# Eight fused layers on one core: work moved across the barriers before the second and third attention, and no announcements of free banks

## The reference

```python
x = x + L0_xattn(layernorm(x), ctx, ctx, Wq, Wk, Wv, Wo)       # 32 heads
x = x + L0_ffn(layernorm(x), c1_w, c2_w, w1, w2t)              # one row per block of 32
x = x + L1_xattn(layernorm(x), ctx, Wq, Wk, Wv, Wo)            # 16 heads of 96, keys: context and x
x = x + L1_ffn(layernorm(x), W, b, lora_A, lora_B)             # Hadamard rotation, LoRA
x = x + L2_xattn(layernorm(x), ctx, mask, Wq, Wk, Wv, Wo, qn, kn)   # 32 heads of 128, q and k normed
x = x + L2_ffn(layernorm(x), weight)                           # quantised to fp8
x = x + L3_xattn(layernorm(x), ctx, ctx)                       # autocorrelation
x = x + L3_ffn(layernorm(x), w1, s1, w2, s2, w3, s3)           # packed 4-bit weights
```

## Time and profile before

| | before |
|---|---|
| median of 3 runs | 1517.04 us (1515.98 to 1517.22) |
| profiled execution, its own time | 1517.68 us |
| its span | 1516.0 us |
| mean granted TensorE clock | 0.968 of full speed |
| TensorE busy | 1394.9 us (92%) |
| VectorE busy | 1078.9 us (71%) |
| ScalarE busy | 763.0 us (50%) |
| GpSimd busy | 719.9 us (47%) |
| DMA | 174.63 MB, q1 59.4% of 16 engines |

### The profile page before, as it was taken

The page is one execution under the profiler, slowest core; times in us unless marked ns, Lnnn a source line. Parts: engine busy times, 40 slices in busy tenths (PEclk is TensorE's granted clock), DMA queues, the critical chain, the costliest instruction groups (busy, mean ns, idle before and its releaser), DMA issues. The chain is left out here.

```text
span 1516.0 us, 31472 instructions
## 1 busy us (share of the span) xinstructions
PE 1394.9 (92%) x11336; PEld 833.2 (55%) x11352; DVE 1078.9 (71%) x2125; ACT 763.0 (50%) x2476; POOL 719.9 (47%) x748
## 2 busy tenths in 40 slices
PE   5898699998999999887999999999999788889998
PEld 4685344445777777434555555555555235434444
DVE  7998555645766766667989888898877779965212
ACT  5777363223434433337766666666665457655111
POOL 4787452002443434845666566665665306734000
PEclk9999699999999999999999999999999899989999
DMA  7999582126999989656876655645544401546000
GB/s 192 184 173 168 129 179 45 32 39 129 188 169 199 170 141 138 125 139 150 154 146 112 116 117 111 140 106 114 105 81 77 123 3 35 124 84 112 19 10 28
DMA packets 524571, 174.63 MB, mean 115 GB/s; under 512 B 482577, under 2 KB 507601, under 8 KB 524417
## 3 DMA queue, kind: packets, MB, share of 16 engines
q1 hardware_dynamic: 524416, 172.62, 59.4%
HBM read 53.27 MB, written 2.10 MB: 37 GB/s over the span
## 5 line engine op out<-in xcount | busy, mean ns | idle before, releaser
L1946 POOL TENSOR_TENSOR a_q_ss<-a_q_ss,half 128x4 f32<-128x4 f32 x64 | 90.2, 1409 | 167.6 <-DVE a_q_ss L1855 83.9
L1768 ACT ACTIVATE a_probs<-a_masked,a_negmax 128x128 f32<-128x128 f32 x256 | 99.6, 391 | 101.5 <-DVE a_negmax L1826 101.5
L67 PE MATMUL bank<-a_wq_hi,xn_pair 128*128 128x512 f16 (+1 forms) x384 | 140.1, 365 | 6.6 <-DVE a_kn L1860 5.2
L1285 POOL TENSOR_TENSOR a_p_hl<-a_probs,a_p_hl 128x512 f16<-128x512 f32 x64 | 74.4, 1164 | 142.0 <-DVE a_p_hl L1209 142.0
L68 PE MATMUL bank<-a_wq_lo,xn_pair 128*128 128x512 f16 (+1 forms) x384 | 139.9, 364 | 0.0
L69 PE MATMUL bank<-a_wq_hi,xn_pair 128*128 128x512 f16 (+1 forms) x384 | 139.8, 364 | 0.0
L67 PE MATMUL bank<-a_wo_hi,a_o_hi 128*128 128x512 f16 x256 | 97.8, 382 | 4.4 <-DVE x_state L1842 3.5
L68 PE MATMUL bank<-a_wo_lo,a_o_hi 128*128 128x512 f16 x256 | 97.6, 381 | 0.0
L69 PE MATMUL bank<-a_wo_hi,a_o_lo 128*128 128x512 f16 x256 | 97.5, 381 | 0.0
L1961 POOL TENSOR_TENSOR a_normal<-a_probs,a_recip 128x512 f32<-128x512 f32 x64 | 90.2, 1410 | 5.0
L716 POOL TENSOR_TENSOR a_p_hl<-a_probs,a_p_hl 128x512 f16<-128x512 f32 x64 | 77.7, 1224 | 23.8 <-DVE a_p_hl L627 17.1
(11 more groups left out here) (467 smaller groups left out, 5028.4 us busy)
## 6 DMA issues: line engine op xcount, KB each, us to landing
a_no<-in_L_xattn_Wo SPq DMA_DIRECT2D x9, 1024.0 KB, 5.7
a_nq<-in_L_xattn_Wq SPq DMA_DIRECT2D x8, 1024.0 KB, 5.7
a_n_wq<-in_L_xattn_Wq SPq DMA_DIRECT2D x4, 768.0 KB, 5.1
a_n_wo<-in_L_xattn_Wo SPq DMA_DIRECT2D x4, 768.0 KB, 5.3
a_nk<-in_L_xattn_Wk SPq DMA_DIRECT2D x9, 256.0 KB, 3.1
a_nv<-in_L_xattn_Wv SPq DMA_DIRECT2D x9, 256.0 KB, 3.1
f_v_hat<-in_L_ffn_w SPq DMA_DIRECT2D x2, 1152.0 KB, 6.2
x_state<-in_x SPq DMA_DIRECT2D x8, 256.0 KB, 5.0
```

Source lines behind the costliest of these rows:

```text
L67: pe.matmul(out, lh, rh, start=start, stop=False)
L1285: pool.tensor_tensor(p_hl[s % PN][:, 1, t, :], probs[unit(s, t) % PROBS][:, :, :].rearrange("p h n -> p (h n)"), p_hl[s % PN][:, 0, t, :], ...
L1768: m = act.activation(probs[s % 2][:, h, :], src, ACT.Exp, bias=negmax[s % 2][:, h:h + 1], accum_out=total[s % 2][:, h:h + 1])
L1946: pool.tensor_tensor(r[:, :], r[:, :], K.half[:, 0:n], ALU.pow).then_inc(root_done.sem, 1)
```

## The change

1. **No announcements.** The counts of `Banks` begin at 0, `wait_free` leaves out the wait of a bank's first use, and all loops that raised `freed` are gone.
2. **First key/value weights of the second attention split a stage ahead.** ScalarE takes the high half and VectorE the low half in step `SPLIT_NEXT` = 25 of `blocks_ffn`. The halves have their tiles already then (`SecondWeights.place`).
3. **First query weights of the second attention loaded a stage ahead,** in step 17 of `blocks_ffn`, right behind the key/value weights, after a wait for the block FFN's last weight piece. Their staging tile (768 KB) serves as the second staging slot of the block FFN's `w1` until then, of which 256 of 384 columns are used.
4. **Statistics of rows 4 to 7** are taken by VectorE at the start of `second_attention` and no longer at the end of `blocks_ffn`.
5. **The queries of batch 1 of the third attention** are made behind the barrier (`MADE` without `("q", 1)`), and the transposes of rows 5 and 6 are issued there, ahead of the loads of the second group's weights.
6. Three classes and functions that nothing calls are deleted.

The diff, cut to its core:

```diff
@@ Banks
     def n_free(self, use, turn=0):
-        return turn * self.per[self.slot[use]] + self.nth[use] + 1
+        return turn * self.per[self.slot[use]] + self.nth[use]
...
     def n_drained(self, use, turn=0):
-        return turn * self.per[self.slot[use]] + self.nth[use] + 2
+        return turn * self.per[self.slot[use]] + self.nth[use] + 1
+
+    def wait_free(self, engine, use, turn=0):
+        if self.n_free(use, turn):
+            engine.wait_ge(self.freed(use), self.n_free(use, turn))
@@ every stage, TensorE's block
-                for banks in (s_bank, o_bank, ring, y_bank):
-                    for freed in banks.freed_sems:
-                        pe.sem_inc(freed, 1)
...
-                    pe.wait_ge(ring.freed(use), ring.n_free(use))
+                    ring.wait_free(pe, use)
@@ second_attention
-                load("wq", 0)
+                load("kv", 1)
...
-                    pe.wait_ge(wlo_done.sem, wlo_done.count(("kv", g, 0)))
+                    if g:
+                        pe.wait_ge(wlo_done.sem, wlo_done.count(("kv", g, 0)))
...
                 for b in later:
+                    K.take_stats(dve, b).then_inc(stats_done, 1)
+                for i, b in enumerate(later):
+                    dve.wait_ge(stats_done, i + 1)
                     m = dve.bn_aggr(mv[:, b, :], K.stats[:, b, :])
@@ wide_attention, SyncE's block
+                for b in first.TURNED_LATE:
+                    turn(b, first.xn_hl[b % first.XB], first.next_in[b % first.XB])
                 for kind in ("wk", "wq"):
                     load(kind, 1)
@@ blocks_ffn
-        nat = {"w1": [front.n1] + ring_of("n1", RING - 1, [P, KT, 2 * P], F32), ...
+        nat = {"w1": [front.n1, nxt.nat["wq"]], ...
...
                     if t == LOAD_NEXT:
+                        sp.wait_ge(wlo_done.sem, wlo_done.count(pieces[-1]))
                         nxt.load_first(sp)
...
+                    if t == SPLIT_NEXT:
+                        nxt.high(act).then_inc(next_hi, 1)
...
+                    if t == SPLIT_NEXT:
+                        dve.wait_ge(next_hi, 1)
+                        nxt.low(dve)
@@ SecondWeights
     def load_first(self, sp):
         self.load(sp, 0, self.first_in["kv"])
+        self.load_queries(sp, 0, self.first_in["wq"])
+
+    def high(self, act):
+        act.wait_ge(self.first_in["kv"], 32)
+        return act.activation(self.kv[0][:, :, :], self.nat["kv"][:, :, :], ACT.Copy, scale=WS)
+
+    def low(self, dve):
+        return dve.scalar_tensor_tensor(self.kv[1][:, :, :], self.nat["kv"][:, :, :], WS, ...
@@ WideFirst
-    MADE = (("k", 0, 0), ("k", 0, 1), ("q", 0), ("q", 1))
+    MADE = (("k", 0, 0), ("k", 0, 1), ("q", 0))
+    TURNED_LATE = (B - 3, B - 2)
@@ rotated_ffn, SyncE's block
                 for b in ahead:
-                    sp.wait_ge(next_lo.sem, next_lo.count(b))
-                    sp.wait_ge(y_bank.filled(b), y_bank.n_filled(b))
-                    turn(b, xn_hl[b % XB], next_in[b % XB])
+                    if b not in first.TURNED_LATE:
+                        sp.wait_ge(next_lo.sem, next_lo.count(b))
+                        sp.wait_ge(y_bank.filled(b), y_bank.n_filled(b))
+                        turn(b, xn_hl[b % XB], next_in[b % XB])
```

More of the change, by code:

```diff
@@ L836, in second_attention @@
         first_group = lambda b: [b] if b in later else []
-        weights_at = lambda t: [(kind, g, i) for g in range(G) for (kind, i), when in W_AT.items() if when == t - g * B]
+        weights_at = lambda t: [(kind, g, i) for g in range(G) for (kind, i), when in W_AT.items()
+                                if when == t - g * B and (kind, g) != ("kv", 0)]
         steps = range(FIRST, END)
@@ L848, in second_attention @@
         whi_done, wlo_done = Steps(sem("whi"), pieces), Steps(sem("wlo"), pieces)
-        mean_done, root_done, blank_done = sem("mean"), sem("root"), sem("blank")
+        stats_done, mean_done, root_done, blank_done = sem("stats"), sem("mean"), sem("root"), sem("blank")
         per_batch = lambda n: Steps(sem(n), batches)
@@ L2219, in load @@
                     kind, q = use
-                    dst = nat[kind][q % RING][:, :, :]
+                    dst = weight(use)[1]
                     if q >= RING:
@@ L2443, in _ @@
                                 add_to_x(u // NT, n)
-                            for n in range(HALF):
-                                stats_of_x(u // NT, n)
+                            if u // NT == 0:
+                                for n in range(HALF):
+                                    stats_of_x(n)
                     for u in live(t):
@@ L2958, in begin @@
     def begin(self, pe):
-        for freed in self.ring.freed_sems:
-            pe.sem_inc(freed, 1)
         pe.wait_ge(self.tab, 80)
@@ L3889, in stage_0_to_1 @@
         K.end_stage()
+        early.place(K, e)
         blocks_ffn(K, front, early)
```

324 lines of the change are left out of this document (72 added, 252 removed).

## The result

| | before | after |
|---|---|---|
| median of the runs | 1517.13 us (4 runs, 1515.98 to 1517.22) | 1504.78 us (4 runs, 1501.28 to 1506.02) |
| ratio, 95% interval | | 0.9917 (0.9899 to 0.9934) |
| profiled execution, its own time | 1517.68 us | 1506.02 us |
| its span, mean granted clock | 1516.0 us, 0.968 | 1504.3 us, 0.974 |
| TensorE busy | 1394.9 us | 1388.1 us |

The total is right. On the two later occasions the same kernel was 0.60% and 0.72% faster by the ratios, 9 and 11 us.

A forecast was written before the change was run, and what follows sets the result against it. TensorE was taken as the bound, so only its starts and waits at barriers count. 3.5 + 0.6 + 2.6 + 1.65 + 0.6 + 1.05 + 1.2 = 11.2 us, from 1517.04 to 1505.8 us; range 1501.0 to 1510.5.

The forecast's parts named there:

- Start of the second attention: Second attention: queries of batch 0 begin at 358.7 instead of 362.24, 3.5 us gained; ends 1.5 and 4.2.
- GpSimd's root and blanks: Second attention's start: a link in the chain to the first queries, taken to last 2.56 us as before.
- the pause ahead of the queries lets the clock fall on the path: Rival, second attention: a fallen clock takes 2.0 off the 3.5 us; total 9.2 us, 1507.8; chance 0.17.
- a clock of 0.50 behind 358 us: Second attention: TensorE at half clock there was listed among the signs that the prediction is wrong.
- the rival of absorption: Attentions: DMA or VectorE pace absorbs half of 3.5 + 4.25 us, 1509.7, or all, 1513.6; chance 0.14.
- End of the rotated FFN: Before the third attention: one product group instead of two, so the barrier opens 2.6 us earlier.
- start of the third attention: Third attention: without 11 announcements of 0.15 us each the whole prologue moves 1.65 us earlier.
- Rotated FFN 0.6, lag attention 1.05, packed FFN 1.2: Starts of these stages: 4, 7 and 8 announcements removed ahead of the first product, 0.15 us each.
- a rival at 0.20: Clock stays up after shorter pauses: packed FFN 2.4, rotated FFN 1.4 us more; total 15.0, 1502.0; chance 0.20.
- both clock rivals: Clock stays up after shorter pauses (1502.0, chance 0.20); clock falls ahead of second attention's queries (1507.8, chance 0.17).
- Quantised FFN: Quantised FFN: four announcements precede TensorE's first transpose, on which the quantisation scale hangs; 0.6 us gained.
- The rival on the other side, late masks: Block FFN: transposes behind the 768 KB load come late, TensorE waits for masks; slower, 1520.2; chance 0.02.

The follow-up runs named there:

- both: Changed kernel with GpSimd's blanks ahead of its wait for means, query-weight load three steps later, statistics ahead of the barrier: 1505.85 us, ratio 0.9932.
- ann_only: Kernel before with only the announcements taken out in all stages: 1507.33 us, ratio 0.9950.
- stats_back: Changed kernel with the statistics of rows 4 to 7 taken at the end of the block FFN again: 1503.30 us, ratio 0.9917.
- order: Changed kernel with GpSimd's blanks before its wait, query-weight load three steps later, statistics behind the first low halves, normalising one step later: 1510.40 us, ratio 0.9969.
- q_back: Changed kernel with the third attention's batch 1 queries and two row transposes ahead of the barrier again: 1507.19 us, ratio 0.9945.
- filler: Changed kernel with 16 needless TensorE products filling the second attention's pause behind the keys and values of batch 1: 1503.99 us, ratio 0.9926.
- after_third: Changed kernel repeated unchanged on a third chip: 1504.69 us, ratio 0.9928.
- ann_back: Changed kernel with the announcements of free banks put back in all stages: 1510.48 us, ratio 0.9964.
- after_again: Changed kernel repeated unchanged as yardstick for the first experiments: 1505.82 us, ratio 0.9940.

## Why the prediction was right, and where it was not

The time came out within 1 us of the forecast, and the count of pauses that was to carry it holds for most of its terms. That it came so close is in part luck: the largest term was missed by 4.7 us in the first trace, and 3.1 us more than forecast in the rotated, lag and packed stages and 1.6 us of chance at the front made up for it.

**Start of the second attention, 3.5 us forecast, -1.2 to 0.7 measured: the step failed, for two reasons.** The chain was named rightly: VectorE 1.05 us behind its last addition, TensorE with it, ScalarE's first halves ended by the blanks. But "GpSimd's root and blanks, 354.74 to 357.30, 2.56 us" was taken from a trace in which both instructions of the root began before VectorE's split (354.74 and 355.06, the split at 355.13). Now VectorE's two splits of the query weights come first (352.94 to 354.73): GpSimd's first instruction, begun 0.17 us behind the first split, ends with it at 353.95, and the second ends 0.9 us behind the second split. Root and blanks last 3.7 us instead of 2.56, so the queries begin 9.08 us behind the last addition (349.21 to 358.29) and not 7.85: 1.2 us lost. All traces fall in line: in the ten where a split was running when the root's instructions began, they took 0.84 (0.76 in `both`) and 1.60 us; in the other four, `before`, `ann_only`, `stats_back` and `order`, 0.23 and 1.04 us. The Trainium skill, SBUF — State Buffer, "Who interferes with whom", says that a VectorE instruction with two inputs in SBUF contends with a GpSimd instruction that reads SBUF, but not with one that only writes it. These traces agree: in `stats_back` the first blanks kept their 0.56 us beside the second split, which has two such inputs. They add that a GpSimd instruction already under way when the split begins keeps its length.

The second reason was on record as a rival at 0.17, "the pause ahead of the queries lets the clock fall on the path", and priced at 2.0 us, a price taken from the 96 key products; that the 12 query products cost nearly the same is a coincidence of their sizes. It had its sign on record too, "a clock of 0.50 behind 358 us". The pause was 3.77 us. In three traces the clock was at 0.50 behind it, in `q_back` not, and `filler` puts the price at 1.9. 3.5 - 1.2 - 1.9 = 0.4 us is the 16.69 - 16.26 of the first trace. A further 1.2 us went in that trace between 396 and 411 us, where the query and key transposes landed 7.8 and 6.6 us after their issue (5.5 and 4.3 in `after_third`, which lost nothing there); in `filler` and `q_back` 0.3 to 0.4 us went. That is the rival of absorption in small. Of the idle time that this rival leaned on, the two pauses are not 11 us but about 7: only 2.15 of the 6.02 us lie behind 354 us.

**The statistics (in that term) bought nothing.** I let them stand in the chain either way and counted the earlier barrier as TensorE's gain. It was no gain: TensorE's earlier start only made its pause longer, and without this part (`stats_back`) the first query product begins at the same distance, 11.72 us, with the clock up. What brought that distance from 14.02 us down to 11.7 can, by elimination, be only parts 2 and 3 of the change, the split and the load a stage ahead: it is 11.7 without part 1 (`ann_back`), without part 4 (`stats_back`) and without part 5 (`q_back`). No run took parts 2 or 3 back by themselves.

**End of the rotated FFN, 2.6, and start of the third attention, 1.65: right.** 2.59 by `q_back`, 1.66 and 1.75 by `ann_only` and `ann_back`, together 4.3 in nearly all traces that have both. These are pauses that keep their place on a chain of other engines. TensorE's clock does not enter it: between 677 and 690 us it was at half for some 7 us in `q_back` and never in `after`, and VectorE's work on the first two key groups starts 4.14 us apart in both. TensorE's own pause was 1.81 us and not about 1.3, because VectorE and not TensorE came last to the barrier.

**Rotated FFN 0.6, lag attention 1.05, packed FFN 1.2: too small, 0.8 to 1.3 and in sum 1.8 to 5.6.** The count of announcements was right, and so were the pauses (0.7 to 1.05 us shorter). What I left at 0 in the forecast, and gave to a rival at 0.20 (for the rotated and the packed FFN), is the clock behind them: from 1336 to 1347 the mean clock was 0.69 against 0.84, and in the lag attention 16 products took 2.02 us in `after` (1241.14) and before

```profile
1249.53 3.75 PE L3074 MATMUL bank<-x_inv,x_q_prod 128*128 128x128 f32 x16 [0.83 <-issue]
```

In the rotated FFN the gain was 1.3 us where the clock stayed at 1.00 (`after`, `after_again`) and 0.8 where it did not (`after_third`). The Trainium skill, TensorE: Matmul & The Clock Gate, Part 1, has the gate's phase differ from run to run; the traces agree: between 1235 and 1347 us the same code spent some 24 us at half clock in `after_again` and 14 in `after_third`, where these stages gave 1.8 and 5.6 us. So both clock rivals came true at different places, and in the first trace the errors cancelled: -4.7 in the second attention, of which 1.9 is the clock, 1.2 the root and 1.2 the late transposes, against +3.1 in the last two stages and the rotated FFN and 1.6 by chance at the front.

**Quantised FFN, 0.6:** 0.6 (6.19 to 6.81 of lead between 1189 and 1202 us). **Block FFN, 0:** the lead at 192 us is -0.3 with announcements (`ann_back`) and between -2.0 and 2.5 without, so nothing is shown. The moved split and the 768 KB load cost nothing that a trace shows: from 230 to 343 us the lead is constant to 0.01 us in each. The rival on the other side, late masks, did not occur.

**What stays open.** Where the spread of some 4 us at 192 us comes from, in code that is the same in nearly all these kernels; at 174 us, the end of the first attention, nearly all of it is there (-2.0 to 1.9). And of the 4.7 us between `after_again` and `after_third`, how much is the clock: `after_again` has about 24 us at half clock between 1235 and 1347 us and `after_third` 14, but none of the runs fixed the clock there.

## What to carry to other kernels

When a barrier is moved forward, ask what fills the time that the first engine gains: work that starts earlier but still waits for the same chain has only traded one pause for another, and the second one may lie on the path. Count a duration from the trace only with what runs beside it in the new order; a GpSimd instruction of 0.23 us took 0.84 when it began behind a VectorE split. And before a chain is shortened at the cost of a later step (`order`), look at what stands on the DMA queue at that step: 6.3 us won at the front were lost behind one transpose.

## What the runs showed of the hardware

- The same pause of 3.77 us was followed by half clock in three executions and by full clock in a fourth. A prediction of such a place has two values, here 16.1 to 16.3 us and 14.4 us to the first queries.
- Where TensorE slows down matters more than for how long: `ann_back` and `stats_back` also have half clock in the second attention, on products with slack. Their first query product begins at the same distance as in the changed kernel (11.7 us), but their queries are ready up to 1.9 us sooner, because the changed kernel had full clock on those products and half clock on the queries.
- A semaphore raise of 51 ns costs 0.15 us each on TensorE's sequencer, and taken together the announcements were worth 7.6 us (6.3 by the stretches) in the kernel before and 3.6 to 4.7 in the changed one. One difference between the two measurements is seen: with the announcements the changed kernel won 3.5 us in the second attention, where without them it won -1.2 to 0.7; 1.9 us of that is the clock.
- A GpSimd instruction of 4 columns that began behind a VectorE split with two inputs in SBUF ended only with it or after it (0.84 us for 0.23); one that began 0.08 us before the split was not lengthened.
- A DMA transpose that landed 2.9 to 3.9 us after its issue with no load just ahead of it landed after 6.9 us when a load of 768 KB was issued 0.5 us before it, and an issue of a transpose stood up to 4.97 us on the queue.
